# Second chunk's projections and two units' maxima ahead of the attention loop, third chunk's in chunk 0, 32 rows per load

## The reference

```python
def proj(W, bias):                       # 16 heads of 16
    return (x @ W + bias).reshape(b, s, H, HD).transpose(0, 2, 1, 3)
scores = einsum('bhqd,bhkd->bhqk', q, k) / sqrt(HD) + slopes * distances   # causal mask
ctx = softmax(scores) @ v
x = x + attn(layernorm(x))               # ctx @ Wo + bo
# feed-forward 256 -> 704 -> 256; weights rounded to -1, 0, 1 by their mean size
x = x + (sigmoid(ln(x) @ w1.T) * (ln(x) @ w2.T)) @ w3.T
```

## Time and profile before

| what | value |
|---|---|
| median of three runs | 731.47 us |
| lowest, highest | 726.93, 732.19 us |
| the profiled execution | 731.91 us |
| its span in the trace | 730.1 us |
| busy in the span | PE 662.2, PEld 382.3, DVE 473.2, ACT 373.0, POOL 109.1 us |
| moved by DMA | 57.66 MB, 79 GB/s in the mean |

### The profile page before, as it was taken

How to read it: one execution, slowest core, us unless ns; L and a number is a source line. 1 busy time by engine, 2 the same in 40 slices (tenths; PEclk the granted TensorE clock), 3 DMA queues, 4 the chain that set the end, 5 groups by cost and what they waited for, 6 DMA issues and landing times.

```text
span 730.1 us, 11113 instructions
## 1 busy us (share of the span) xinstructions
PE 662.2 (91%) x3710; PEld 382.3 (52%) x3710; DVE 473.2 (65%) x1194; ACT 373.0 (51%) x768; POOL 109.1 (15%) x139
## 2 busy tenths in 40 slices
PE   2688869999999989989999999997899999899997
PEld 1344535545565555545555565553455555366487
DVE  4367746767777764658877777784788787511175
ACT  1514533465554432646655545475476675476621
POOL 5645100030011111120001212003000000031000
PEclk9969965799999986999999999999899999899999
DMA  8783967557441410745234133247153120011000
GB/s 264 148 143 127 166 97 107 89 158 157 65 75 32 88 31 18 179 128 81 53 61 74 31 68 51 45 86 162 32 79 61 32 45 0 1 40 39 1 16 29
DMA packets 39789, 57.66 MB, mean 79 GB/s; under 512 B 7156, under 2 KB 16884, under 8 KB 39732
## 3 DMA queue, kind: packets, MB, share of 16 engines
q1 hardware_dynamic: 39732, 56.96, 38.7%
HBM read 41.87 MB, written 14.80 MB: 78 GB/s over the span
## 4 chain that ended last, share of the span: by engine, by line
PE 72%; DVE 11%; DMA 8%; issue 3%; SPq 2%; ACT 2%; POOL 1%; ACTq 0%; POOLq 0%; DVEq 0%
PE pS L906 18%; PE pO L919 17%; PE pM L886 17%; PE pW L861 5%; DVE pM L1058 3%; PE pW L870 3%; PE pS L909 2%; DMA qst<-parts 2%; DVE pm L1055 2%; PE pW L807 2%; PE pW L847 2%; DMA ctx_dram<-ctx_raw 2%; PE pW L813 2%; PE pS L870 1%; DMA rden_dram<-dens 1%
## 5 line engine op out<-in xcount | busy, mean ns | idle before, releaser
L757 ACT ACTIVATE probs<-pS 128x512 f32<-128x512 f32 (+3 forms) x640 | 314.0, 535 | 284.0 <-PE pS L909 142.1
L1055 DVE TENSOR_REDUCE pm<-pM 128x1 f32<-128x512 f32 x384 | 244.5, 684 | 88.0 <-PE pM L886 87.5
L886 PE MATMUL pM<-kst,qst 96*128 96x512 f32 (+3 forms) x640 | 251.2, 421 | 31.6 <-DMA qst<-parts 13.3
L906 PE MATMUL pS<-qst,kst 98*128 98x512 f32 (+3 forms) x640 | 259.9, 423 | 3.6 <-DMA qst<-mT 2.8
L906 PEld LDWEIGHTS pS<-qst,kst 98*128 98x128 f32 x640 | 124.5, 197 | 141.5 <-ACT probs L757 107.2
L1058 DVE CUSTOM_DVE_ANT_0 pM<-pM,mask 128x128 f32<-128x128 f32 (+3 forms) x256 | 120.7, 515 | 74.1 <-PE pM L886 73.4
L886 PEld LDWEIGHTS pM<-kst,qst 96*128 96x128 f32 x640 | 128.0, 205 | 64.7 <-DVE pm L1055 20.8
L919 PE MATMUL pO<-probs,vals 128*17 128x512 f32 (+3 forms) x1280 | 154.9, 556 | 0.0
L909 PE MATMUL pS<-maskb,identb 128*128 128x128 bf16 x256 | 61.6, 242 | 0.0
L618 POOL TENSOR_TENSOR rstd<-ve,mhalf 128x4 f32<-128x4 f32 (+1 forms) x9 | 8.5, 947 | 285.3 <-DVE ve L971 285.3
L919 PEld LDWEIGHTS pO<-probs,vals 128*17 128x17 f32 x1280 | 21.5, 96 | 43.9 <-issue 30.2
(11 more groups left out here) (145 smaller groups left out, 421.0 us busy)
## 6 DMA issues: line engine op xcount, KB each, us to landing
kst<-parts SPq DMA_DIRECT2D x160, 128.0 KB
parts<-qk_hl SPq DMA_DIRECT2D x32, 256.0 KB, 3.0
qst<-parts SPq DMA_DIRECT2D x64, 128.0 KB, 5.7
ctx_dram<-ctx_raw SPq DMA_DIRECT2D x15, 256.0 KB, 5.9
xin<-in_L_attn_x SPq DMA_DIRECT2D x5, 512.0 KB, 5.1
out<-work SPq DMA_DIRECT2D x8, 256.0 KB, 2.2
work<-ctx_dram SPq DMA_DIRECT2D x7, 256.0 KB
work<-rden_dram SPq DMA_DIRECT2D x7, 256.0 KB
```

What stands on the lines that cost most here:

```text
L757: nc.scalar.activation(probs[:, n % PSLOTS, q0:CH], pS[:, n % SBANKS, q0:CH], ACT.Exp)\
L886: pe.matmul(max_bank(x)[:, 0:N], qst[0:R_MAX, u % QSLOTS, h, t * P:(t + 1) * P], kst[0:R_MAX, n % KSLOTS, h, 0:N], start=True, stop=True). ...
L906: ins = pe.matmul(pS[:, n % SBANKS, q0:CH], kst[0:R_END, sl, h, b:b + P], qst[0:R_END, u % QSLOTS, h, q0:CH], start=True, stop=not is_diag ...
L1055: nc.vector.tensor_reduce(dst, bank, AX.X, ALU.max).then_inc(max_free, 1)
```

## The change

Chunk 1's k, q and v are all made in the head, and the head takes the turns of two units (`HEAD_MAX`), with chunk 1's last k, q and two v groups set among them (`head_after`). Chunk 2's xT, k and q move to steps 3 to 8 and its v to steps 16 and 17; chunk 3's xT, k and q move to steps 19 to 24, its v to 48 and 49. The layer norms that these need start at steps 0 and 16, in place of 12 and 43. The turns of unit 4 start at step 9 in place of 10, those of units 2 and 3 earlier too. The stacks lose their filler rows (`R_MAX` is 66 instead of 96), and `parts` is laid out so that one DMA loads 32 rows: three DMAs for a key piece in place of five, three for a query slot in place of four, with the same bytes. The tables put key loads up to four steps earlier. GpSimd makes most of its constants after the first layer norm instead of ahead of it, and ScalarE takes its three sums of the raw weights among the first projections.

```diff
@@ -39,11 +39,11 @@
     R_ALIBI = 4 * HD
-    R_MAX = 96
+    R_MAX = R_ALIBI + 2
     R_END = R_MAX + 2
...
     SBANKS, MBANKS = 3, 3
-    K_DMAS, Q_DMAS, PART_DMAS = 5, 4, 2
+    K_DMAS, Q_DMAS, PART_DMAS = 3, 3, 2
@@ -69,13 +69,12 @@
-        v = u - 1
-        return first_step[u] - (3 if n_steps[v] > TPC else 2)
-    LOADS_AT, TURNS_AT = 6, 8
+        return first_step[u] - (5 if u < NHG else 3)
+    LOADS_AT, TURNS_AT = 2, 6
     def turns_start(u):
-        s0 = swap_step(u - 1) if u >= 2 else 0
+        s0 = max(swap_step(u - 1), first_step[u - 2] + 1) if u > HEAD_MAX else 0
         c, hg = units[u]
@@ -84,6 +83,7 @@
+    HEAD_MAX = 2
     weight_groups = [("w", i, k) for i in range(3) for k in range(2)]
@@ -99,14 +99,14 @@
     for c in range(NCH):
-        lst = pre_groups(c + 1) if c + 1 < NCH else []
-        if c == 0:
-            lst = lst[4:] + [None] * 3
+        lst = [] if c == 0 else pre_groups(c + 1)[-2:] if c < NCH - 1 else []
+        if c + 2 < NCH:
+            lst = lst + [None] * (3 - len(lst)) + pre_groups(c + 2)[:-2]
         lst = lst + (weight_groups if c == 0 else [None] * (POST_AT[c] - len(lst)) + post_groups(c - 1))
...
                 side[phase0[c] + i] = g
-    LN_AT = {0: 12, 1: 27, 2: -9, 3: -9}
+    LN_AT = {0: 0, 1: 0, 2: -9, 3: -9}
     TERN_STEPS = range(0, 6)
@@ -136,7 +136,7 @@
     step_swap = [None] * NS
-    for u in range(1, NU):
+    for u in range(HEAD_MAX, NU):
         a, b = turns_start(u), swap_step(u)
@@ -154,7 +154,9 @@
-    bank_use = [("turn", 0, k) for k in range(n_turns(0))] + [("swap", 0)]
+    bank_use = []
+    for u in range(HEAD_MAX):
+        bank_use += [("turn", u, k) for k in range(n_turns(u))] + [("swap", u)]
     for s in range(NS):
@@ -164,8 +166,9 @@
-    head_first, head_last = pre_groups(0) + pre_groups(1)[:2], [("gamma",)] + pre_groups(1)[2:4]
+    head_first, head_last = pre_groups(0) + pre_groups(1)[:4], pre_groups(1)[4:] + [("gamma",)]
     head_groups = head_first + head_last
+    head_after = {(0, 5): head_last[0], (0, 11): head_last[1], (1, 3): head_last[2], (1, 9): head_last[3]}
@@ -192,7 +195,7 @@
-    parts = nc.dram_tensor("parts", (2, NCH, KT, 2, P, CH), F32, kind="Internal").ap()
+    parts = nc.dram_tensor("parts", (2, NCH, H, 2, HD, CH), F32, kind="Internal").ap()
     alibi_parts = nc.dram_tensor("alibi_parts", (2, H, T), F32, kind="Internal").ap()
@@ -397,7 +400,8 @@
                 for part in range(2):
-                    sp.dma_start(parts[w, g[1], g[2], part, :, :], qk_hl[:, i % 2, part, :])\
+                    sp.dma_start(parts[w, g[1], g[2] * P // HD:(g[2] + 1) * P // HD, part, :, :],
+                                 qk_hl[:, i % 2, part, :])\
                         .then_inc(parts_out[i % 2], 16)
@@ -405,10 +409,9 @@
-            def part_rows(w, c, hg, part):
-                m, r0 = hg * G * HD // P, hg * G * HD % P
-                return parts[w, c, m, part, r0:r0 + G * HD, :].rearrange("(h d) n -> d h n", d=HD)
+            def part_rows(w, c, hg):
+                return parts[w, c, hg * G:(hg + 1) * G, :, :, :].rearrange("h p d n -> (p d) h n")
@@ -420,9 +423,9 @@
                 hg = units[v][1]
-                for b in range(4):
-                    sp.dma_start(kst[b * HD:(b + 1) * HD, n % KSLOTS, :, :].bitcast(F32),
-                                 part_rows(1, i, hg, b % 2)).then_inc(k_in[n % KSLOTS], 16)
+                for b in range(2):
+                    sp.dma_start(kst[b * 2 * HD:(b + 1) * 2 * HD, n % KSLOTS, :, :].bitcast(F32),
+                                 part_rows(1, i, hg)).then_inc(k_in[n % KSLOTS], 16)
                 sp.dma_start(kst[R_ALIBI:R_ALIBI + 2, n % KSLOTS, :, :].bitcast(F32),
@@ -434,9 +437,10 @@
                     sp.wait_ge(q_rows, v + 1)
-                for b, part in enumerate((0, 1, 1, 0)):
-                    sp.dma_start(qst[b * HD:(b + 1) * HD, v % QSLOTS, :, :].bitcast(F32),
-                                 part_rows(0, c, hg, part)).then_inc(q_in[v % QSLOTS], 16)
+                src = part_rows(0, c, hg)
+                for d0, s0, n in ((0, 0, 2 * HD), (2 * HD, HD, HD), (3 * HD, 0, HD)):
+                    sp.dma_start(qst[d0:d0 + n, v % QSLOTS, :, :].bitcast(F32), src[s0:s0 + n, :, :])\
+                        .then_inc(q_in[v % QSLOTS], 16)
@@ -516,23 +520,28 @@
             load_q(0)
+            load_k(1)
+            load_q(1)
             store_parts(("k", 0, 1))
             store_parts(("q", 0, 1))
-            load_k(1)
-            load_q(1)
-            load_m(0)
             load_k(2)
             load_q(2)
-            for g in head_last[1:]:
-                store_parts(g)
+            load_x(2)
+            store_parts(("k", 1, 0))
+            store_parts(("q", 1, 0))
+            load_k(3)
+            store_parts(("k", 1, 1))
+            store_parts(("q", 1, 1))
+            load_m(0)
+            load_m(1)
...
             k_at, q_at = {}, {}
-            for n in range(3, len(pieces)):
+            for n in range(4, len(pieces)):
                 v, i = pieces[n]
                 c = units[v][0]
-                s = max(0, first_step[v - 1] - 5)
+                s = max(0, first_step[v - 1] - 9)
                 if n >= KSLOTS:
@@ -566,8 +575,8 @@
                         load_x1(c)
-                if ph == 3 and c + 2 < NCH:
-                    load_x(c + 2)
+                if ph == 5 and c + 3 < NCH:
+                    load_x(c + 3)
                 if ph == 4 and c >= 1:
@@ -646,7 +632,6 @@
-                link(nc.gpsimd.memset(qst[R_ALIBI:R_MAX, n, :, :].bitcast(F32), 0.0))
                 nc.gpsimd.memset(qst[R_ALIBI:R_ALIBI + 2, n, :, :].bitcast(F32), 1.0).then_inc(q_rows, 1)
@@ -657,18 +642,45 @@
+            link(nc.gpsimd.memset(mhalf[:, :], -0.5))
+            link(nc.gpsimd.memset(minus1[:, :], -1.0))
+            for i in range(2):
+                ins = nc.gpsimd.memset(w_rows[i][FROWS[FT - 1]:P, FT - 1, :], 0.0)
+            ins.then_inc(pad_ok, 1)
+            pool.wait_ge(pad_ok, 1)
+            link(nc.gpsimd.memset(ident[:, :], 0.0))
+            nc.gpsimd.affine_select(out=ident[:, :], in_=ident[:, :], compare_op=ALU.not_equal, fill=1.0,
+                                    base=0, pattern=[[-1, P]], channel_multiplier=1).then_inc(const_ok, 1)
+            pool.wait_ge(const_ok, 1)
             key_rows(0)
+            query_rows(0)
             power(1)
-            query_rows(0)
+            pool.wait_ge(xn_ok, 1)
+            link(nc.gpsimd.tensor_copy(identb[:, :], ident[:, :]))
+            link(nc.gpsimd.memset(mask[:, :], 0.0))
+            link(nc.gpsimd.affine_select(out=mask[:, CH - P:CH], in_=mask[:, CH - P:CH], compare_op=ALU.is_ge,
+                                         fill=NEG, base=0, pattern=[[-1, P]], channel_multiplier=1))
+            link(nc.gpsimd.memset(maskb[:, :], 0.0))
+            link(nc.gpsimd.affine_select(out=maskb[:, :], in_=maskb[:, :], compare_op=ALU.is_ge, fill=NEG,
+                                         base=0, pattern=[[1, P]], channel_multiplier=-1))
+            nc.gpsimd.memset(ones, 1.0).then_inc(const_ok, 1)
+            pool.wait_ge(const_ok, 2)
+            key_rows(1)
+            query_rows(1)
             split_lo(("k", 0, 0))
+            split_lo(("q", 0, 0))
             power(2)
-            split_lo(("q", 0, 0))
+            key_rows(2)
             split_lo(("k", 0, 1))
+            query_rows(2)
             split_lo(("q", 0, 1))
-            for n in range(1, QSLOTS):
-                key_rows(n)
-                query_rows(n)
-            for g in head_last[1:]:
+            key_rows(3)
+            for g in pre_groups(1)[2:6]:
                 split_lo(g)
@@ -680,8 +692,8 @@
                     split_hidden(g)
-                if 0 <= s - 2 < KSLOTS - QSLOTS:
-                    key_rows(QSLOTS + s - 2)
+                if s < KSLOTS - 4:
+                    key_rows(4 + s)
                 if ph == 2 and c >= 1:
@@ -766,18 +778,20 @@
             act.wait_ge(wsum_ok, 1)
-            for g in head_first:
-                if g[0] != "v":
-                    side_op(g)
-            act.wait_ge(raw_in, 80)
-            for i in range(3):
+            def abs_sum(i):
+                if i == 0:
+                    act.wait_ge(raw_in, 80)
                 act.wait_ge(wsum_ok, i + 1)
...
                     .then_inc(wsum_ok, 1)
-            for g in head_last[1:]:
-                side_op(g)
+            abs_after = {("q", 0, 0): 0, ("k", 0, 1): 1, ("q", 0, 1): 2}
+            for g in head_groups:
+                if g[0] in ("xT", "k", "q"):
+                    side_op(g)
+                if g in abs_after:
+                    abs_sum(abs_after[g])
             for s, (u, j) in enumerate(steps):
@@ -924,11 +938,14 @@
                 side_group(g)
-            for k in range(n_turns(0)):
-                max_turn(0, k)
-            swap_max(0)
-            for g in head_last:
-                side_group(g)
```

(21 more changed lines are left out.)

18 lines of the change are left out of this document (removed).

## The result

| kernel | median of 4 runs | lowest, highest | profiled execution (span) | clock in the mean |
|---|---|---|---|---|
| before | 731.83 us | 726.93, 733.39 | 731.91 (730.1) | 0.937 |
| after | 828.23 us | 816.75, 839.41 | 816.75 (815.0) | 0.83 |

The changed kernel is slower: ratio 1.119, 95% interval 1.113 to 1.125. The forecast was 710 us. The profiled execution is one of the two faster ones of the four, and every ratio here is taken over the faster executions of both kernels. All that follows is read against its span.

A forecast was written before the change was run, and what follows sets the result against it. TensorE bounds chunks 1 and 2; head and chunk 0 wait, and waits lower its clock. Terms 0 (head and chunk 0), -10.5, -10 and -1.5 sum to -22 against 731.9 us: 710 us, range 696 to 731.

The forecast's parts named there:

- Filler rows cost TensorE nothing: All turns and scores: dropping filler changes no TensorE time, as an instruction is as long as its columns; costed at nothing.
- B: Rival: chunk 1's low-clock patch stays or one like it appears, and 32-row loads are no faster; 721 us, chance 0.29.
- C: Rival, slower: clock falls in step 3 behind a late layer norm, stays at 1.2 GHz to step 13; 741 us, chance 0.09.
- Head and chunk 0 together end at 139 us: Head plus chunk 0: they end where they end now, net 0, between -13 and +16 us.
- Head: Start to first scores: first turn at 33.1 us, head ends at 59 us, +7.5 (+4 to +11).
- chain of stores: Head: unit 0's maxima queue behind chained projection stores, last issued at about 56 us; maxima land at about 59.
- Chunk 0: Steps 0 to 15, walked by their waits: 80 us against 87.2 now, -7; bounds 70 and 92 us.
- Step 3's wait for the normalise: Chunk 0: chunk 2's xT is queued behind the layer norm, so TensorE idles some 6 us.
- Step 9's wait: Chunk 0: unit 4's query rows wait behind three key pieces; the wait moves here, about 6 us (now 7.23).
- Chunks 1 and 2: Chunk 1 -10.5 us (fewer turns, low clock behind step 43's layer norm gone); chunk 2 -10 us (six groups fewer).
- Loads of 32 rows: Key and query loads: 200 GB/s taken against 143 for 16 rows; the skill page's ratio would give 260.
- Chunk 3: The 8.30 us wait for the spread denominators shortens by faster key loads: -1.5 us (0 to -3).

The follow-up runs named there:

- a_rows96: The changed kernel with the filler rows put back (R_MAX 96), all else as changed: 737.29 us, ratio 1.010 to the kernel before.
- a_m_early: The changed kernel with filler to row 126 and load_m(0) issued ahead of the stores of chunk 1's projections: 729.12 us, ratio 0.999.
- a_r96_load16: The changed kernel with filler back (R_MAX 96) and loads of 16 rows, so the change of order alone: 747.82 us, ratio 1.014.
- a_q_first: The changed kernel with filler to row 126, load_m(0) ahead of the stores, and load_q ahead of load_k in SP's loop: 713.25 us, ratio 0.974.
- b_q_first: The kernel before with loads of 32 rows, filler to row 126 and load_q ahead of load_k: 709.30 us, ratio 0.971.
- b_rows66: The kernel before with its filler rows taken out (R_MAX 66), nothing else changed: 821.41 us, ratio 1.119.
- a_q_first_r66: a_q_first with the filler taken out again (66 and 68 rows): 829.91 us, four runs from 786.01 to 834.58.

## Why the prediction was wrong

**The step that failed** is, as it stood there: "Filler rows cost TensorE nothing, since its instruction is as long as its columns", and "Costed at nothing". The premise holds (190 ns and 0.40 us for 66 or 126 rows at full clock). The conclusion doesn't: in chunk 3 the rows decide how long TensorE stays at 1.2 GHz once it has fallen. Priced on the kernel before, by itself, this term is nearly +90 us; priced on the changed kernel, between a_rows96 and after, it is +80 us by the ratios and +72 by the spans of the profiled runs. Its parts by the spans are +4.4 in chunk 0, +3.6 in chunk 1, nothing in chunk 2 and +64.6 in chunk 3. None of the rivals had it: B and C had the clock falling elsewhere, but all of them took the length of a low stretch from the earlier trace rows, where the stacks had 96 rows. The error was to carry a duration over while the change took away one of its conditions. Nothing in the trace of before showed that condition, since every turn and score there had the same rows. So it couldn't be read. It could have been bounded, though: an edit that touches each of 1280 matmuls was costed with one number and no upper end.

**The rest of the change**, read in a_rows96, is no gain either: span 742.8 us, 12.7 over before, where the forecast's terms sum to -22. So a second step failed, "Head and chunk 0 together end at 139 us": in a_rows96 they end at 178, +39 us where the forecast had nothing and +16 as its upper bound. By stages, forecast and measured:

| part | forecast | a_rows96 |
|---|---|---|
| head | +7.5 (+4 to +11) | +17.1 |
| chunk 0 | -7 (-17 to +5) | +22.2 |
| chunk 1 | -10.5 | -11.2 |
| chunk 2 | -10 | -10.3 |
| chunk 3 | -1.5 | -5.2 |

- **Head, too low by 10 us.** Two things add up. The first turn starts at 37.95 us (kernel after) and not at 33.1, and not behind its query rows: TensorE was still making chunk 1's first k and q groups, which now stand ahead of the turns. From there to unit 1's swap it is 23.8 us, for 23.4 in the forecast.

```profile
36.63 1.88 PE L821 MATMUL pS<-xnT,wq_s 128*128 128x512 f32 x4
37.95 0.97 PE L900 MATMUL pM<-kst,qst 66*128 66x128 f32 x3
```

  And the chain of stores was named and under-priced. ScalarE's two waits for a landing are 10.24 and 8.72 us, where I had counted 4 to 5 us for a pair with its landing; and unit 0's maxima, behind all stores, kept TensorE 5.61 us. a_m_early moves that one DMA and gets 6.0 us back, which shows this part; the first is read from the timeline and was not tried.
- **Chunk 0, wrong in sign.** The walk by waits was right in kind and too short in every part. From the first scores of steps 0, 4, 5, 9 and 16 in a_rows96, with the forecast in brackets: steps 0 to 3 22.7 us (19), step 4 3.6 (3), steps 5 to 8 28.6 (17), the rest 54.6 (41). Steps 5 to 8 are the largest miss. Their first turn waits 4.48 us for 3, four projection groups and not three stand among them, two of these at the low clock (3.15 and 3.54 us), and a rounding of 2.25 us, which the walk had ahead of step 4, holds TensorE for 2.20. Step 3's wait for the normalise is 1.17 us, not 6. Step 9's wait is 12.60 in the changed kernel for 6: from the opening of the slot (119.6 us) to the first turn (136.39) it is 16.8 us, where I had counted 11 and a landing, and TensorE had 4.2 us of other work in it, where I had counted 6.5.

  The clock was 0.63 over the whole chunk in a_rows96, low from 65 to 95 and from 130 to 175 us. This is near to rival C, which I gave 0.09: low clock through the early steps, though it begins at the loop's first wait, for the maxima, and not in step 3, and is mostly up again from 105 to 128 us. That C was priced at 741, where a_rows96 has 742.8 in its span and 737.3 in the median, is luck. C had +21 us for head and chunk 0 and -12 behind them, and measured are +39 and -27.
- **Chunks 1 and 2, right.** There the bound was TensorE and the matmuls left. Steps 50 on are plain now (48 and 49 still have a v group each), 3.06 us from one group of weighted values to the next where the earlier trace rows have 4.77 and 7.04 (kernel after):

```profile
334.19 1.05 PE L933 MATMUL pO<-probs,vals 128*17 128x512 f32 x8
337.25 1.05 PE L933 MATMUL pO<-probs,vals 128*17 128x512 f32 x8
```

  The low patch behind the layer norm of step 43 is gone, too: after 270 us chunk 1 has no wait of a microsecond, and its clock is 1.00 in a_rows96 and 0.97 in the changed kernel.
- **Loads of 32 rows, right in their rate.** 200 GB/s were taken, and some 207 are seen, against 143 for 16 rows. The Trainium skill, "SBUF — State Buffer", section "Door 1: The DMA port swizzle", makes it 189 after 104; the gain here is 1.4 times, less than its 1.8, so the 260 GB/s worked out from it were too many. What the faster loads are worth in the changed kernel is not shown (a_r96_load16).
- **Chunk 3, right in kind.** TensorE's wait for the denominators fell from 7.06 to 2.60 us in a_rows96, and the stage by 5.2 us, for a forecast of 1.5.

With its waits mended (a_q_first, 713.25 us) the staging of the changed kernel does no better than the staging of the old one with the same loads and rows (b_q_first, 709.30). By stages of the profiled runs, a_q_first against b_q_first is head +10.3, chunk 0 +6.9, chunk 1 -3.6, chunk 2 -10.0, chunk 3 -4.1 us: what is gained in chunks 1 to 3 is given back ahead of them.

**What stays open.** Why the rows matter, and why so much more in chunk 3 than in chunk 1. The runs show that their number does and their content hardly, that one instruction's length doesn't change, and that it isn't even in the rows. They do not show what in the chip weighs them. In after, b_rows66 and a_q_first_r66 the clock came back at about 678, 703 and 716 us; in the latter two this was right behind a `wo` group, of 128 rows, in after it was not, so that a group of full rows ends the stretch is only a guess. Chunk 2 of the changed kernel has 66 rows too and stays at 1.00 for 179 us: few rows alone don't bring the clock down.

## What to carry to other kernels

Treat the number of contracted rows as part of what keeps TensorE's clock up. Filler up to 128 rows cost no time in an instruction and was worth 1.3% in the kernel before (in the changed kernel it was not told from filler to 98); taking the filler out cost 12%. When a change touches every matmul, price it on the granted clock and not on the instruction's length alone, and don't take the length of a low stretch from a trace in which the matmuls had another shape. In a queue that loads for several consumers, put what is waited for next (here 512 KB of query rows) ahead of what is merely early (keys): this took 2% off the changed kernel and nothing that could be measured off the kernel before.
